# Scan stage of a fused transformer kernel: the decays' product with its operands turned round, in two fp32r parts made by GpSimd

## The reference, cut to what matters

```
dt = softplus(dt_raw + dt_bias);  A = -exp(A_log)
dA  = dtc * A                                   # per token and head, 4 heads
cum = cumsum(dA, axis=2)                        # inside a chunk
seg = cum[:, :, :, None, :] - cum[:, :, None, :, :]
decay  = where(tril, exp(seg), 0)
scores = einsum('bcin,bcjn->bcij', Cc, Bc)
att    = scores[..., None] * decay * dtc
y_intra = einsum('bcijh,bcjhp->bcihp', att, xc)
... state carried from chunk to chunk, skip, gate silu(z), RMS norm, output projection
```

## Time and profile before

| | |
|---|---|
| Time, median of 3 runs | 5127.16 us (5111.26 to 5134.68) |
| Profiled execution, span from first to last instruction | 5138.9 us (no other time of it is given) |
| PE, DVE, ACT, POOL busy over the span | 4706.1, 4275.5, 3471.8, 1377.0 us |
| Mean granted TensorE clock | 0.936 |
| Scan stage | from about 3.61 to 4.51 ms of the span, its turns from 3.70 ms on |

### The profile page before, as it was taken

How to read it: one execution, slowest core, us unless ns; L and a number is a source line. 1 busy time by engine, 2 the same in 40 slices (tenths; PEclk the granted TensorE clock), 3 DMA queues, 4 the chain that set the end, 5 groups by cost and what they waited for, 6 DMA issues and landing times. The chain is left out here.

```text
span 5138.9 us, 109366 instructions
## 1 busy us (share of the span) xinstructions
PE 4706.1 (92%) x35413; PEld 2589.8 (50%) x35413; DVE 4275.5 (83%) x6882; ACT 3471.8 (68%) x6677; POOL 1377.0 (27%) x1279
## 2 busy tenths in 40 slices
PE   5869999999999999999999689999599999955998
PEld 4723333333333333333333267777366666645887
DVE  5779999999999999999999768878677877775554
ACT  2428888888888888888888523223377877734554
POOL 1111111111111111111111133333234443435776
PEclk8969999999999999999999889999699999956999
DMA  4931222212222122221222211111100000044442
GB/s 153 349 67 35 52 52 46 43 35 53 52 46 43 35 53 51 46 43 38 50 54 43 71 40 37 41 45 37 53 21 27 25 23 28 21 156 164 166 160 92
DMA packets 236717, 340.13 MB, mean 66 GB/s; under 512 B 60215, under 2 KB 170034, under 8 KB 227612
## 3 DMA queue, kind: packets, MB, share of 16 engines
q1 hardware_dynamic: 220032, 275.39, 22.3%
q0 software_dynamic: 16192, 58.43, 3.1%
HBM read 205.62 MB, written 136.18 MB: 67 GB/s over the span
## 5 line engine op out<-in xcount | busy, mean ns | idle before, releaser
L719 DVE TENSOR_REDUCE at_mxp<-at_ps_m 128x2 f32<-128x1024 f32 x2092 | 2524.4, 1221 | 70.2 <-PE at_ps_m L772 47.3
L692 ACT ACTIVATE at_prob<-at_ps_s 128x512 f32<-128x512 f32 x4100 | 2227.3, 596 | 323.5 <-PE at_ps_s L762 299.7
L782 PE MATMUL at_ps_o<-at_prob,at_vs 128*32 128x256 f32 x16384 | 1313.1, 392 | 13.9 <-ACT at_osum L698 13.9
L762 PE MATMUL at_ps_s<-at_qs,at_ks 51*128 51x512 f32 x4100 | 1036.7, 500 | 2.7 <-ACT at_prob L692 2.7
L772 PE MATMUL at_ps_m<-at_ks,at_qs 49*128 49x512 f32 x4184 | 859.0, 406 | 49.8 <-DMA at_ks<-t_alibi 34.4
L762 PEld LDWEIGHTS at_ps_s<-at_qs,at_ks 51*128 51x128 f32 x4100 | 384.6, 183 | 853.3 <-ACT at_prob L692 852.8
L782 PEld LDWEIGHTS at_ps_o<-at_prob,at_vs 128*32 128x32 f32 x16384 | 322.9, 108 | 778.2 <-issue 389.7
L564 POOL TENSOR_TENSOR at_total<-at_total,at_minus 128x16 f32<-128x16 f32 x65 | 189.6, 2917 | 1128.4 <-DMA at_total<-at_osum 1128.4
L772 PEld LDWEIGHTS at_ps_m<-at_ks,at_qs 49*128 49x128 f32 x4184 | 403.7, 190 | 73.7 <-DVE at_mxp L719 38.0
L67 DVE TENSOR_TENSOR ex_hidc<-ex_hid,ex_hidc 128x512 fp32r<-128x512 f32 x128 | 158.5, 1250 | 169.6 <-ACT ex_hid L2550 169.6
L1222 PE MATMUL mi_ps_f<-mi_w,mi_act 128*128 128x256 f32 x1024 | 260.1, 399 | 17.4 <-DVE mi_acc L1072 17.1
(11 more groups left out here) (317 smaller groups left out, 6161.6 us busy)
## 6 DMA issues: line engine op xcount, KB each, us to landing
t_parts<-pr_parts SPq DMA_DIRECT2D x64, 512.0 KB, 6.4
ex_w<-in_fw SPq DMA_DIRECT2D x32, 1024.0 KB, 7.4
at_ks<-t_parts SPq DMA_DIRECT2D x102, 256.0 KB
t_buf<-at_blank POOLq DMA_DIRECT2D x64, 384.5 KB, 3.2
at_qs<-t_parts SPq DMA_DIRECT2D x96, 256.0 KB
at_vs<-t_v SPq DMA_DIRECT2D x17, 1024.0 KB, 4.8
ex_rest<-t_buf SPq DMA_DIRECT2D x16, 1026.0 KB, 5.2
t_v<-pr_vaug SPq DMA_DIRECT2D x64, 256.0 KB, 5.6
```

The costliest lines, as they stand in the source:

```text
L692: nc.scalar.activation(prob[0 if up is None else (t + 1) % 2][:, j, :], ps_s[bank][:, :], ACT.Exp).then_inc(s_read, 1)
L719: nc.vector.tensor_reduce(out[:, s4, k + i, 2 * pair:2 * pair + 2], ps_m[i][:, :, :], AX.X, ALU.max).then_inc(mx_read, 1)
L762: nc.tensor.matmul(ps_s[bank][:, :], ks[s][a:a + QROWS, j // 2, t1 * P:(t1 + 1) * P], qs[s][a:a + QROWS, j // 2, c * T:(c + 1) * T], start ...
L782: last = nc.tensor.matmul(ps_o[32 * j:32 * j + 32, q0:q1], vs[s][:, t, 32 * j:32 * j + 32], prob[t % 2][:, j, q0:q1], start=(t == 0 and ha ...
```

## The change

The product is computed with the operands in the other places: the constant triangle `lower`, cut once to fp32r (`lowerc`), is stationary, and `upper` scaled by dA is the moving operand, 512 columns for all four heads at once. fp32r holds fewer bits, so dA is first split into two fp32r parts (`step_parts`: four small POOL instructions), and POOL makes a scaled `upper` from each (`segment_mask`: two 128x512 multiplies with fp32r output). PE adds two matmuls into the bank. ACT's `segment_mask` and its calls go. DVE makes `lowerc` before its weight rounds, and PE's weight rounds wait for it.

```diff
+                def step_parts(h):
+                    pool.drain()
+                    nc.gpsimd.tensor_scalar(dA_big[:, :, :], dA[h][:, :, :], 4097.0, None, ALU.mult)
+                    pool.drain()
+                    nc.gpsimd.tensor_tensor(dA_off[:, :, :], dA_big[:, :, :], dA[h][:, :, :], ALU.subtract)
+                    pool.drain()
+                    nc.gpsimd.tensor_tensor(dAc[h][0][:, :, :], dA_big[:, :, :], dA_off[:, :, :], ALU.subtract)
+                    pool.drain()
+                    lower_part(nc.gpsimd, dAc[h][1][:, :, :], dA[h][:, :, :], dAc[h][0][:, :, :])
+                    pool.drain()
+
+                def segment_mask(h, s, used):
+                    if used is not None:
+                        pool.wait_ge(a_done, used + 1)
+                    for c in range(2):
+                        last = nc.gpsimd.tensor_tensor(segc[s % 2][c][:, :, :], upper[:, :].unsqueeze(1).to_broadcast([P, NH, P]),
+                                                       over_h(dAc[h][c][:, s, :].bitcast(F32)), ALU.mult)
+                    last.then_inc(seg_set, 1)
...
                         gate(i, h, 0, old)
                         second_root(i + 2)
+                        segment_mask(h, 3, place(turn, "seg1")[0])
                         if c == 0:
                             weigh_rows(b, i)
                         softplus_argument(i + 1)
                         softplus_series(i + 1, 1 - h)
                         gate(i, h, 1, old)
+                        step_parts(1 - h)
+                        segment_mask(1 - h, 0, place(turn, "seg2")[0])
                         gate(i, h, 2, True)
+                        segment_mask(1 - h, 1, place(turn, "seg3")[0])
                         gate(i, h, 3, True)
+                        segment_mask(1 - h, 2, place(turn, "seg0")[0])
...
                 softplus_series(0, 0)
                 second_root(1)
+                pool.wait_ge(const_in, NCONST)
+                step_parts(0)
+                segment_mask(0, 0, None)
+                segment_mask(0, 1, None)
+                segment_mask(0, 2, place(None, "seg0")[0])
                 pool.wait_ge(w_read, RND)
-                pool.wait_ge(const_in, NCONST)
...
                 dve.wait_ge(const_in, NCONST)
+                nc.vector.tensor_copy(lowerc[:, :], lower[:, :]).then_inc(lower_cut, 1)
...
-                def segment_mask(n, h, s, used):
-
-                    act.wait_ge(dA_done, n + 1)
-                    if used is not None:
-                        act.wait_ge(a_done, used + 1)
-                    for k in range(NH):
-                        last = nc.scalar.activation(segm[s % 2][:, k, :], lower[:, :], ACT.Copy, scale=dA[h][:, s, k:k + 1])
-                    last.then_inc(seg_set, 1)
...
                     pe.wait_ge(seg_set, i * SUB + s + 1)
-                    for k in range(NH):
-                        last = nc.tensor.matmul(bank[:, k * P:(k + 1) * P], segm[s % 2][:, k, :], upper[:, :], start=True, stop=True)
+                    for c in range(2):
+                        last = nc.tensor.matmul(bank[:, :], lowerc[:, :], segc[s % 2][c][:, :, :].rearrange("p h c -> p (h c)"), start=(c == 0), stop=(c == 1))
                     last.then_inc(a_done, 1)
...
                 pe.wait_ge(const_in, NCONST)
+                pe.wait_ge(lower_cut, 1)
                 pe.wait_ge(setup_v, 2)
```

More of the change, by code:

```diff
@@ L1319, in scan_phase @@
         two = lambda name, shape: [sb(f"{name}{h}", shape) for h in range(2)]
-        segm, decay, att = two("segm", [P, NH, P]), two("decay", [P, NH, P]), two("att", [P, NH, P])
+        decay, att = two("decay", [P, NH, P]), two("att", [P, NH, P])
+        segc = [[sb(f"segc{h}{c}", [P, NH, P], F32R) for c in range(2)] for h in range(2)]
+        dAc = [[sb(f"dAc{h}{c}", [P, SUB, NH], F32R) for c in range(2)] for h in range(2)]
+        dA_big, dA_off = sb("dA_big", [P, SUB, NH]), sb("dA_off", [P, SUB, NH])
+        lowerc = sb("lowerc", [P, P], F32R)
         sm, btw, ex = two("sm", [P, P]), two("btw", [P, NH, NS]), two("ex", [P, 3, SUB, NH])
@@ L1348, in scan_phase @@
         conv_done, silu_done, nabs_done, ez_done, dA_done = sem("conv_done"), sem("silu_done"), sem("nabs_done"), sem("ez_done"), sem("dA_done")
-        seg_set, att_done, g_done = sem("seg_set"), sem("att_done"), sem("g_done")
+        seg_set, lower_cut, att_done, g_done = sem("seg_set"), sem("lower_cut"), sem("att_done"), sem("g_done")
         sc_done, sc_read, in_done, in_read = sem("sc_done"), sem("sc_read"), sem("in_done"), sem("in_read")
@@ L1471, in batch @@
                         h = c % 2
+                        turn = (i, c)
                         old = c > 0 or not first
@@ L1827, in _ @@
                 normed(None, 1, ("vT0", "vT1"))
-                segment_mask(0, 0, 0, None)
-                segment_mask(0, 0, 1, None)
                 sums(None, 0)
                 decays(None, 0, 0, False)
-                segment_mask(0, 0, 2, place(None, "seg0")[0])
                 skip_inputs(None, 0, 0, 0, False)
@@ L1842, in batch @@
                         steps(turn)
-                        segment_mask(i, h, 3, place(turn, "seg1")[0])
                         decays(turn, i, 1, old)
@@ L1858, in batch @@
                         decays(turn, i, 3, True)
-                        segment_mask(i + 1, 1 - h, 0, place(turn, "seg2")[0])
                         projected(turn, h, 0)
@@ L1864, in batch @@
                         decays(turn, i + 1, 0, True)
-                        segment_mask(i + 1, 1 - h, 1, place(turn, "seg3")[0])
                         gates(turn, 1 - h, 2)
@@ L1881, in batch @@
                         projected(turn, h, 3)
-                        segment_mask(i + 1, 1 - h, 2, place(turn, "seg0")[0])
                         skip_inputs(turn, i + 1, 1 - h, 0, True)
```

## The result

5223.45 us, the median of 4 runs (5210.48 to 5234.36), against 5123.8 us for the kernel before (now with a fourth run; the three above gave 5127.16); ratio 1.0195, 95% interval 1.0174 to 1.0217. The forecast was 5229 us and slower: 102 us more, where the medians now lie 99.65 apart. The profiled execution spans 5221.4 us, 82.5 us more than its counterpart; the scan stage alone, from its first to its last instruction, takes 997.71 us where it took 891.67. The rest of the program differs by some 24 us the other way (82.5 less 106.0) though nothing there was changed, and over the 13 traces of this document that rest takes 4217 to 4247 us, with 4247 in the trace before.

The account below looks back on a forecast made before the run. PE alone set the 48.5 us turns, with hardly 0.15 us of room after POOL's chain. The terms made +6.3 us a turn, 101 us in 16 turns, 102 with the prologue: 5127 + 102 = 5229 us, range 5172 to 5275.

Parts of the forecast that it names:

- per-turn sum: Scan turn: PE -1.8, ScalarE -0.4, waits +5.8, clock +2.2, port +0.5, together +6.3 us a turn over 16 turns.
- PE's product: Decays' product on PE: two fp32r matmuls replace four fp32 products, 0.45 us saved four times, -1.8 us a turn.
- The chain: POOL's work from second root to mask s = 0 (mask s = 3, softplus, gate 1, splits, mask): 23.2 us.
- The waits: PE waits for POOL 2.6 us at gate 1 and 3.1 us at the mask for s = 0; +5.8 us a turn.
- The clock: PE's granted clock falls after the two waits in each scan turn: +2.2 us a turn (0 to 3.3).
- ScalarE: ScalarE loses 16 activations of 128x128 a scan turn: -0.4 us a turn (0 to -1.0).
- The port: POOL's eight new multiplies slow DVE's instructions beside them, mostly absorbed: +0.5 us a turn (0 to 4).
- lock-out rule: A two-SBUF-input DVE instruction and an SBUF-reading POOL one exclude each other; a mask multiply could delay a step its full length.
- Rival C: The port decides: POOL's masks hold up DVE in the scan, +4 in place of +0.5 us a turn; 5285 us, chance 0.12.
- The prologue: Before the scan turns: PE's weight transposes wait for DVE's triangle copy, first product's mask comes sooner; +1 us (-3 to +5).
- Rival B: The clock doesn't answer to the waits, PE's work between them keeps it up: +4.1 us a turn, 5194 us, chance 0.16.

Follow-up runs that it names:

- e7: Kernel before with PE's new fp32r product alone, its moving operand a constant triangle, so dA is left out of the decays; 5124.94 us, ratio 1.0014.
- e8: Changed kernel with five discarded fp32 matmuls of 256 columns on PE ahead of each of its two waits; 5171.23 us, ratio 1.0096.
- e6: Kernel before with POOL's new splits and mask multiplies added, into tiles that nobody reads; 5173.22 us, ratio 1.0128.
- e3: Changed kernel with the mask for s = 3 ahead of gate 0 and the product of s = 0 in the old form by ScalarE; 5143.38 us, ratio 1.0044.
- e4: e3 with the weighing of the output rows also moved ahead of gate 0; 5137.57 us, ratio 1.0030.
- e10: e4 with two discarded fp32 matmuls of 256 columns on PE ahead of gate 1's transposes; 5121.43 us, ratio 1.0007.
- e5: Kernel before with only the weighing of the output rows moved ahead of gate 0; 5100.5 us, ratio 0.9971.

## Why the prediction was right

Against the per-turn sum, as measured in the 15 turns:

- PE's product: forecast -1.8, measured -1.73 (e7). Right.
- The chain: forecast 23.2 us after the root, measured 22.8: mask 1.96 for 2.54, softplus 15.4 for 15.2, gate 1 1.2, splits with their drains 2.0 for 1.7, mask 2.3 for 2.54. A mask multiply takes 1.04 us, not the 1.27 of the gate; that was the nearest row, not the right one. Its tile in the kernel after:

```profile
L1473 POOL TENSOR_TENSOR sc_segc<-sc_upper,sc_dAc x134: 1032/1040/1493, 3672.8 to 4598.1; 128x512 fp32r<-128x512 f32 x134
```

- The waits: forecast 2.6 and 3.1 us, measured 2.43 and 2.75, released as said. In the weighing turn I had 9.5 us and there are 7.1 (the two lines below): I counted PE's earlier arrival as 1.35 us (0.9 is left after the root), the masks too long, and PE does the transposes and sums between the waits at the low clock, in 2.2 us in place of 1.05, so 1.1 us of the second wait became slow work. PE's idle time grew by 4.7 us a turn in place of 5.8.

```profile
4184.76 1.09 PE L2011 MATMUL sc_ps_a<-ident,sc_g 128*128 128x128 f32 x4 [5.42 <-POOL sc_g L1489]
...
4188.59 1.22 PE L1959 MATMUL sc_ps_a<-sc_segc,sc_lowerc 128*128 128x512 f32 x2 [1.65 <-POOL sc_segc L1473]
```

- The clock: forecast +2.2, and this term was too small. PE's busy time rose by 1.75 us a turn though 1.73 us of work went: 3.5 us are lost that neither waits nor work explain, against 2.2 + 0.5 - 0.4 in my sum. e8 shows that most of it is the clock: with low-clock time back near that of before, its mean turn is 54.72 us where after has 57.41, 2.7 us less. The other 0.8 us no run separates. I had priced one spell a turn; there are two, since the one at the start of the turn became both commoner and longer.
- ScalarE: forecast -0.4. Its busy time fell by 4.4 us a turn (588.33 to 522.53 in 15 turns), but no run has this edit alone, so what it is worth stays open.
- The port: forecast +0.5. DVE's convolution steps got slower, mean 816 to 923 ns, and att 730 to 835 ns: 9 x 0.107 + 4 x 0.105 = 1.4 us a turn, beside 16 us a turn in which DVE does nothing. Only the first part is POOL's load as such: in e6, which has all of it, the convolution steps have a mean of 922 ns too, but att has 727. DVE's lines for the convolution before and after:

```profile
L1572 DVE SCALAR_TENSOR_TENSOR sc_cv<-sc_xc,sc_conv_w,sc_cv 128x512 f32<-128x512 f32 x238 | 186.4, 816 | 15.1 <-issue 7.0
```
```profile
L1605 DVE SCALAR_TENSOR_TENSOR sc_cv<-sc_xc,sc_conv_w,sc_cv 128x512 f32<-128x512 f32 x210 | 186.9, 923 | 13.4 <-issue 6.0
```

The longest step is 2.05 us by its tile, 1.81 before: 1.3 us over the median, about one multiply of POOL, which agrees with the lock-out rule that the prediction cited from the Trainium skill (SBUF — State Buffer, Who interferes with whom). Rival C's price for it was far too high here.
- The prologue: forecast +1, measured +0.6 from the scan's first instruction to the first carried product (71.48 us before, 72.08 after). The first product's wait fell from 2.69 us to 0.21 as forecast, but the carried product behind it then waited 2.68 us for DVE's first state, where it had waited 0.98.

So the mechanism was right, and the total came out as close as it did, 6.3 a turn for 6.5, by some luck, because two errors cancelled: waiting 1.1 too high, the clock and the rest 1.2 too low. The turns without row weighing were to last 54 to 56 us and last 55.5 to 57.5; the weighing ones were to last 60 to 62 and last 59.1 to 61.6. Rival B's arithmetic for a clock that stays up (+4.1 a turn) is nearly what e8 gives (+3.7); only the clock doesn't stay up by itself.

The 15 to 20 us by which e3 and e4 stay over the kernel before go with the low clock. Their turns without a spell last 48.0 to 48.4 us, no more than the 48.5 of before; the turns with spells are the long ones. DVE's busy time rose as well (43.70 us in one of e3's turns), but as busy a DVE didn't hold this turn of e10 up:

```profile
4066.90:4114.90 48.00, 48.00 (x233) 31.49 (x232) 43.67 (x99) 36.15 (x85) 31.01 (x38) 1.00 0.09 26
```

What stays open: why e4's later turns nearly all begin with a spell at the low clock, far from their wait; the 0.8 us a turn above; and a mask multiply in e6 that reads nothing DVE contends for wasn't tried.

## What to carry to other kernels

An engine that is 40% busy can still have no room: look for the stretch of its program order that ends in another engine's wait, and put new work in front of what that stretch begins with, not inside it. When a tuned loop is bound by PE, quicker work on PE is worth at most the room that the next engine's chain leaves (here half of it, and in the end nothing that the times show). And price a new wait of PE with the clock: the wait here cost 4.7 us a turn and the slower clock some 2.7 more (e8).

## What the runs showed of the hardware

- Work that is thrown away can pay: five discarded fp32 matmuls of 256 columns ahead of each wait took 52 us off the program.
- Waits of some 0.9 us at one place in most turns and a shorter product came with a mean clock of 0.94 in the 15 turns (e4), where the kernels with the old product have 0.97 and 0.98 (before, e5), in spells at another place of the turn; with 0.86 us of filler in the wait it was 0.98 again (e10).
- A microsecond at the low clock cost 0.5 us where PE alone sets the turn (50.18 for 48.50 us, with one spell of 3.4 us by its clock records) and, an estimate from e8 against after, some 0.3 us where POOL's chain sets part of the turn: 144 us less of it in 16 turns, 2.7 us less a turn.
- A 128x512 multiply on POOL took 1.04 us in the median with the mask's operands, of which one repeats over heads and one over columns and the output is fp32r, and 1.27 us with two full ones and an fp32 output.
